# A fused scan, expert and quantised feed-forward kernel: ten entries per batch for the second scan's projections, and the first gate and the routing in one block

## What is computed

```python
# layer 0
x = x + silu(layernorm(x)) * ssm(ctx)        # the scan reads the context, not x
logits = layernorm(x) @ gate_w.T             # 16 experts, 4 chosen per token
x = x + sigmoid(...) * shared_ffn(xn) + sum_e coef_e * expert_e(xn)
# layer 1
x = x + silu(layernorm(x)) * ssm(ctx)        # a second scan of the same context
x = x + quantised_ffn(layernorm(x))

def ssm(h):                                  # per batch of 512 steps, 512 channels, 16 states
    u     = silu(causal_conv4(in_proj(h)))
    dt, B, C = split(x_proj(u))
    delta = softplus(dt_proj(dt) + bias)
    state = state * exp(delta * A) + delta * u * B
    y     = sum_n(state * C) + D * u
```

## Time and profile before

| | |
|---|---|
| median of 3 runs | 2226.88 us |
| the profiled execution | 2235.07 us, its span 2233.3 us |
| mean granted TensorE clock | 0.869 of 2.4 GHz |
| busy: TensorE, VectorE, GpSimd, ScalarE | 74%, 79%, 60%, 52% of the span |
| first gate | 648.4 to 725.9 us |
| routing | 727.7 to 788 us |
| block with the 168 slots | from 789.8 us |

### The profile page before, as it was taken

The page is one execution under the profiler, slowest core; times in us unless marked ns, Lnnn a source line. Parts: engine busy times, 40 slices in busy tenths (PEclk is TensorE's granted clock), DMA queues, the critical chain, the costliest instruction groups (busy, mean ns, idle before and its releaser), DMA issues. The chain is left out here.

```text
span 2233.3 us, 27174 instructions
## 1 busy us (share of the span) xinstructions
PE 1658.5 (74%) x8502; PEld 960.6 (43%) x8502; DVE 1757.4 (79%) x2275; ACT 1152.6 (52%) x1765; POOL 1341.3 (60%) x648
## 2 busy tenths in 40 slices
PE   4575766756638548999799998999989990016999
PEld 1122222222218525676467654666456660003554
DVE  2999999999955836998589867888588884856886
ACT  5676776766632014443444435555455550734776
POOL 2679878789952003887078945888268883652111
PEclk8688988879965569999999998999989995557999
DMA  7536546355542820000000442444424227640000
GB/s 256 196 137 214 178 159 211 135 190 194 175 146 76 160 68 11 10 10 15 34 10 1 149 140 102 148 165 161 156 102 160 82 76 295 182 155 6 20 25 29
DMA packets 127145, 264.63 MB, mean 118 GB/s; under 512 B 44547, under 2 KB 48387, under 8 KB 121795
## 3 DMA queue, kind: packets, MB, share of 16 engines
q1 hardware_dynamic: 93890, 184.24, 24.6%
q0 software_dynamic: 11520, 37.76, 5.7%
q10 hardware_dynamic: 21600, 40.90, 4.9%
HBM read 180.41 MB, written 82.44 MB: 118 GB/s over the span
## 5 line engine op out<-in xcount | busy, mean ns | idle before, releaser
L476 POOL TENSOR_TENSOR ssm_hs<-ssm_hs,ssm_Cs 128x1024 f32<-128x1024 f32 x128 | 313.9, 2461 | 89.5 <-DVE ssm_hs L443 89.5
L476 POOL TENSOR_TENSOR moe_hs<-moe_hs,moe_Cs 128x1024 f32<-128x1024 f32 x128 | 301.5, 2355 | 98.4 <-DVE moe_hs L443 97.5
L443 DVE TENSOR_TENSOR_SCAN moe_hs<-moe_dA,moe_bu 128x1024 f32<-128x1024 f32 x128 | 292.5, 2285 | 20.0 <-ACT moe_dA L357 10.2
L466 POOL TENSOR_TENSOR moe_U<-moe_U,moe_hs 128x1024 f32<-128x1024 f32 x128 | 302.2, 2361 | 5.9
L443 DVE TENSOR_TENSOR_SCAN ssm_hs<-ssm_dA,ssm_bu 128x1024 f32<-128x1024 f32 x128 | 291.6, 2278 | 0.1
L290 PE MATMUL ssm_pY<-ssm_hs,ssm_ident 128*128 128x512 f32 x512 | 275.5, 666 | 4.2 <-POOL ssm_hs L476 4.2
L1238 PE MATMUL moe_pgu<-moe_xsh,all_Wreg 128*128 128x256 f16 x1408 | 255.5, 280 | 12.8 <-DVE moe_hsl L1483 11.3
L1288 PE MATMUL moe_pgu<-all_Wreg,moe_xth 128*128 x1280 | 243.7, 313 | 0.0
L699 POOL TENSOR_TENSOR ssm_wlo<-ssm_wst,ssm_whi 128x1360 f16<-128x1360 f32 x64 | 190.3, 2973 | 45.7 <-ACT ssm_wst L635 45.7
L357 ACT ACTIVATE ssm_dA<-ssm_dlt,ssm_A 128x511 f32<-128x511 f32 x256 | 168.0, 710 | 63.2 <-DVE ssm_hs L443 60.0
L1238 PE MATMUL moe_pgu<-moe_xsl,all_Wreg 128*128 128x256 f16 x704 | 197.1, 280 | 0.0
(11 more groups left out here) (246 smaller groups left out, 3490.6 us busy)
## 6 DMA issues: line engine op xcount, KB each, us to landing
ssm_wst<-in_w_all SPq DMA_DIRECT2D x64, 680.0 KB, 5.0
w_hi<-ssm_whi SPq DMA_DIRECT2D x64, 340.0 KB, 2.3
w_lo<-ssm_wlo SPq DMA_DIRECT2D x64, 340.0 KB, 3.1
y_d<-moe_yo ACTq DMA_DIRECT2D x80, 256.0 KB, 3.1
all_Wreg<-w_hi SPq DMA_DIRECT2D x16, 1088.0 KB, 5.8
all_Wreg<-w_lo SPq DMA_DIRECT2D x16, 1088.0 KB, 8.7
ssm_Cs<-c_d SPq DMA_DIRECT2D x64, 256.0 KB, 5.4
gate_Y<-y_ssm ACTq DMA_DIRECT2D x8, 1024.0 KB, 9.2
```

Source lines behind the costliest of these rows:

```text
L443: self.nc.vector.tensor_tensor_scan(self.hs[:, j, :, :].rearrange("p k t -> p (k t)"), self.dA[:, q, :, :].rearrange("p k t -> p (k t)"), ...
L466: self.nc.gpsimd.tensor_tensor(Y, Y, self.hs[:, j, :, :], ALU.add).then_inc(self.acc_done, 1)
L476: self.nc.gpsimd.tensor_tensor(self.hs[:, j, :, :], self.hs[:, j, :, :], self.Cs[:, i:i + 1, :].to_broadcast([P, HC, L]), ALU.mult)\
```

## The change

Two parts.

1. PRO goes from 5 to 10, so PER is 42, the entries are 168 and each slot has one. Entries 0 to 3 hold one channel chunk each, entry 4 the Silu, entry 5 the x-projection, entries 6 and 7 the dt matmuls with Abs and Relu, and from 6 to 9 the rest by halves. The x-projection writes into pB instead of the first bank of `bu`; the convolution waits for GpSimd's sums by single steps.
2. `gate` with l = 0 and `routing` become one block, `gate_and_routing`. The constants are loaded at the start of it, with the weights of four chunks of the shared expert; the other chunks' loads stand between the stores of xn. G has 8 tiles instead of 16. The one-hot tiles and their source are f16. The table of the slots' experts comes from two small matmuls. `gate` stays for the second layer.

```diff
+    def bank_x(self):
+        return self.pw[0] if self.alone else self.pB[:]
+    def bank_dt(self, b, c):
+        return self.bank(b, c + 1 if self.alone else c)
...
-        if c == n - 1:
+        if c == n - 1 and self.alone:
             pe.wait_ge(self.bc_split, 5 * (b + 1))
-            if self.alone:
-                pe.wait_ge(self.cf_rdy, b + 1)
+            pe.wait_ge(self.cf_rdy, b + 1)
...
             if not self.alone:
-                act.wait_ge(self.acc_done, b * STEPS + R)
+                act.wait_ge(self.acc_done, b * STEPS + R - 3 + c // 2)
...
-        PRO = 5
+        PRO = 10
...
-                    if at == 0 or at == 1:
-                        S.pe_in(pe, b, 2 * at)
-                        S.pe_in(pe, b, 2 * at + 1)
+                    if at is not None and at < KC:
+                        S.pe_in(pe, b, at)
...
-                    if at == 2:
+                    if at == 5:
                         S.pe_x(pe, b)
-                    if at == 3:
-                        S.pe_dt(pe, b, 0)
-                        S.pe_dt(pe, b, 1)
+                    if at in (6, 7):
+                        for c in range(2):
+                            S.pe_dt(pe, b, 2 * (at - 6) + c)
...
+                    if at == 6:
+                        S.act_dt(act, b)
+                    if at in (7, 8):
+                        S.act_e(act, b, at - 7)
+                    if at in (8, 9):
+                        S.act_ln(act, b, at - 8)
                     if g >= 2:
                         y_evac(g - 2)
...
+                    if at is not None and at < KC:
+                        S.act_conv(act, b, at)
+                    if at == 2 and b:
+                        S.store_y(act, y_ssm, b - 1)
+                    if at == 3 and b + 1 < B:
+                        S.load_ctx(act, b + 1)
+                    if at == 4:
+                        S.act_u(act, b)
+                    if at in (6, 7):
+                        for c in range(2):
+                            S.act_z(act, b, 2 * (at - 6) + c)
...
+                    if at is not None and at < KC:
+                        S.dve_conv(dve, b, at)
+                    if at == 6:
                         S.dve_split(dve, b)
+                    if at in (7, 8):
+                        S.dve_t(dve, b, at - 7)
+                    if at in (8, 9):
+                        S.dve_delta(dve, b, at - 8)
+                        S.dve_du(dve, b, at - 8)
```

In the new block:

```diff
+def gate_and_routing(nc, d, X, y_ssm, r):
...
-        G = m.sb("G", [P, TT, L])
+        G = m.sb("G", [P, TT // 2, L])
...
-        ohp = m.sb("ohp", [P, 4, P])
-        ohs = m.sb("ohs", [P, 4, NSTEP])
+        ohp = m.sb("ohp", [P, 4, P], F16)
+        ohs = m.sb("ohs", [P, 4, NSTEP], F16)
...
+        colh = m.sb("colh", [P, P], F16)
...
+                for c in range(4):
+                    shared(c)
+                for i in range(TT):
+                    sp.wait_ge(xn_rdy, i + 1)
+                    sp.dma_start(r["xn_d"][i * P:(i + 1) * P, :], xn[:, i % 4, :]).then_inc(xn_out[i % 4], 16)
+                    if i + 4 < CSH:
+                        shared(i + 4)
...
+                    if i >= TT // 2:
+                        act.wait_ge(yg_rdy, i - TT // 2 + 1)
...
+                V.tensor_copy(r["first"][:], start[0:1, :])
+                own(V.tensor_scalar(begun[:, 0, :], start[:], tok[:, 0:1], None, ALU.is_le))
+                own(V.tensor_tensor(begun[:, 1, :], begun[:, 0, :], turn[:], ALU.mult))
+                V.reduce_sum(sew[:], begun[:], AX.X).then_inc(se_rdy, 1)
                 for g in range(TT * TOPK):
...
+                    V.tensor_scalar(ohp[:, g % 4, :], colh[:], pp[:, i, k:k + 1], None, ALU.is_equal)
+                    V.tensor_scalar(ohs[:, g % 4, :], colh[:, 0:NSTEP], stf[:, i, k:k + 1], tok[:, i:i + 1],
                                     ALU.is_equal, ALU.mult).then_inc(oh_rdy, 1)
...
+                dve.wait_ge(tab_rdy, 1)
+                V.tensor_copy(r["tab"][0:1, :, :], ptab[:, 0:2 * NSTEP].rearrange("p (a n) -> p a n", a=2))
...
+                pe.wait_ge(se_rdy, 1)
+                for q in range(2):
+                    mm = nc.tensor.matmul(ptab[:, q * NSTEP:(q + 1) * NSTEP], sew[:, q:q + 1], ident[:, 0:NSTEP],
+                                          start=True, stop=True)
+                mm.then_inc(tab_rdy, 1)
```

More of the change, by code:

```diff
@@ L717, in gate @@
+def gate_and_routing(nc, d, X, y_ssm, r):
+    with ExitStack() as ctx:
+        m = Mem(nc, ctx, "gate0")
         ident = m.sb("ident", [P, P])
@@ L750, in gate @@
         lg_out = m.sem("lg_out")
+        tri = m.sb("tri", [P, P])
+        ones = m.sb("ones", [P, P])
+        e_of = m.sb("e_of", [P, E])
+        thr = m.sb("thr", [P, TT])
+        col = m.sb("col", [P, P])
+        tok = m.sb("tok", [P, TT])
+        ex = m.sb("ex", [P, TT, E])
+        mx = m.sb("mx", [P, TT])
+        sm = m.sb("sm", [P, TT])
+        ri = m.sb("ri", [P, TT])
+        i8 = m.sb("i8", [P, TT, 8], U32)
+        idf = m.sb("idf", [P, TT, 8])
+        oh = m.sb("oh", [P, TOPK, TT, E])
+        M = m.sb("M", [P, TT, E])
+        base = m.sb("base", [P, TT, E])
+        cnt = m.sb("cnt", [P, TT, E])
+        off = m.sb("off", [P, TT + 1, E])
+        cmp = m.sb("cmp", [P, E, TT])
+        nt = m.sb("nt", [P, E])
+        incl = m.sb("incl", [P, E])
+        start = m.sb("start", [P, E])
+        one_e = m.sb("one_e", [P, E])
+        pos = m.sb("pos", [P, TT, TOPK])
+        posi = m.sb("posi", [P, TT, TOPK], I32)
+        sti = m.sb("sti", [P, TT, TOPK], I32)
+        stf = m.sb("stf", [P, TT, TOPK])
+        pp = m.sb("pp", [P, TT, TOPK])
+        ohp = m.sb("ohp", [P, 4, P], F16)
+        ohs = m.sb("ohs", [P, 4, NSTEP], F16)
+        turn = m.sb("turn", [P, E])
+        begun = m.sb("begun", [P, 2, E])
+        sew = m.sb("sew", [P, 2])
+        colh = m.sb("colh", [P, P], F16)
+        flat = [t[:].rearrange("p k t -> p (k t)") for t in pt]
+        pr_, pc, pi, ptab = flat[0][:, 0:TT * E], flat[1][:, 0:TT * E], flat[2][:, 0:NSTEP], flat[3][0:1, :]
+        r_loaded = m.sem("r_loaded")
+        mx_rdy = m.sem("mx_rdy")
+        e_rdy = m.sem("e_rdy")
+        se_rdy = m.sem("se_rdy")
+        tab_rdy = m.sem("tab_rdy")
+        m_rdy = m.sem("m_rdy")
+        rk_rdy = m.sem("rk_rdy")
+        oh_rdy = m.sem("oh_rdy")
+        oh_used = m.sem("oh_used")
+        step = m.sem("step")
+        fin = m.sem("fin")
         with nc.Block() as block:
@@ L1063, in _, with second, evac @@
                 dve.wait_ge(oh_used, TT * TOPK)
                 own(V.tensor_copy(r["idx"][:], pi[:]))
+            @block.scalar
+            def _(act):
+                for b in range(B):
+                    own = slice(b * KC, (b + 1) * KC)
+                    act.dma_start(Y[:, own, :], y_ssm.rearrange("(i p) t -> p i t", p=P)[:, own, :]).then_inc(y_in[b], 16)
+                act.wait_ge(eps_rdy, 1)
+                act.wait_ge(mv_rdy, TT)
+                nc.scalar.activation(sd[:, 0, :], mv[:, :, 1], ACT.Sqrt, bias=eps[:]).then_inc(sd_rdy, 1)
+                act.wait_ge(ln_rdy, 1)
+                for i in range(TT):
+                    if i >= TT // 2:
+                        act.wait_ge(yg_rdy, i - TT // 2 + 1)
+                    nc.scalar.activation(G[:, i % (TT // 2), :], X[:, i, :], ACT.Silu, bias=nmr[:, 0, i:i + 1],
+                                         scale=rstd[:, 0, i:i + 1]).then_inc(g_rdy, 1)
+                def second(b):
+                    own = slice(b * KC, (b + 1) * KC)
+                    act.wait_ge(mv_rdy, TT + (b + 1) * KC)
+                    nc.scalar.activation(sd[:, 1, own], r["mv"][:, own, 1], ACT.Sqrt, bias=eps[:]).then_inc(sd_rdy, 1)
+                def evac(b):
+                    for c in range(KC):
+                        i = b * KC + c
+                        act.wait_ge(tn_rdy, i + 1)
+                        if i >= 4:
+                            act.wait_ge(lg_rdy, i - 3)
+                        nc.scalar.copy(xT[:, i % 4, :, :], pn[i % 2][:]).then_inc(xT_rdy, 1)
+                second(0)
+                second(1)
+                for b in range(B):
+                    evac(b)
+                    if b + 2 < B:
+                        second(b + 2)
+                act.wait_ge(lg_rdy, TT)
+                nc.scalar.copy(r["logit"][:], plog[:, :, 0:E + 1]).then_inc(lg_out, 1)
+                act.wait_ge(mx_rdy, 1)
+                nc.scalar.activation(ex[:], ex[:], ACT.Exp).then_inc(e_rdy, 1)
+                nc.scalar.activation(r["sig"][:], r["logit"][:, :, E], ACT.Sigmoid).then_inc(fin, 1)
@@ L1524, in _ @@
                         S.dve_bu(dve, b, half, s)
-                    if at == 4:
-                        for h in range(2):
-                            S.dve_t(dve, b, h)
                     if g <= 0 and slot:
@@ L1943, in bass_program @@
         }
-        gate(nc, 0, d, X, y_ssm, r)
         with nc.sbuf_tensor("all_Wreg", [P, 2 * CSH * WC], F16) as Wreg:
```

(2 more changed lines are left out.)

360 lines of the change are left out of this document (151 added, 209 removed).

## The result

The changed kernel takes 2217.66 us, the median of 5 runs (2214.28 to 2223.25), beside 2228.55 for the kernel before (5 runs, 2226.09 to 2229.55): a ratio of 0.9948, interval 0.9933 to 0.9962.

What follows compares the result with a forecast made beforehand. It took TensorE to bound expert slots, with TensorE and VectorE both near their limit in shared slots. Entries +0.4 and gate and routing -1.1 sum to -0.7 us, so 2226 us was predicted, range 2211 to 2241.

Steps and rivals of the forecast that it cites:

- the tail of the first projections: Shared slots, wait after the last projection slot's tanh until the first scan: 12.4 us.
- the casts in a run of scans: Shared scan runs: two casts of 0.69 and two residual adds of 0.74 per 11 slots add 0.26 us per slot.
- what the held stores cost: Gate: xn stores wait behind chunk loads in SyncE's queue, delaying the logits by 11.7 us, bounds +7 to +15.
- the walk: 168-slot block, costed from scan to scan: +5.8, -25.9, +22.7 and -2.2 us, together +0.4.
- 31 x 5.04 = 156.3: Run of 32 scans in shared slots: 31 gaps of 4.79 plus 0.26 us for casts and adds.
- The gaps: Ten projection entries between batches' scans: 68.9 us in shared slots, 85.4 from batch 1 to 2, 91.8 in expert slots.
- 31 x 6.51 = 201.8: Run of 32 scans in expert slots: 31 gaps of 6.51 us, with TensorE full.
- tails vanish: Rival for the projections' tails: chains overlap better than walked, -23 us, 2204 at full price, 2212 at half; chance 0.18.
- The long scan runs hold VectorE and GpSimd above 5.04: Rival for shared scan runs: at 5.3 us per slot +17, 2243; decides from 5.1 on; chance 0.20.
- 20 empty slots were what let VectorE and GpSimd recover: Shared phase: removing the empty slots offsets some 30 us less of projection stalls.
- Store 7 is issued at 716: Gate, SyncE's queue: 28.3 us of load issue and eight stores of 0.5 put store 7 there, landing 2.5 later.
- the stores aren't held up: Rival for the gate: SyncE issues loads faster than in the old routing, -11.7 us, 2214; chance 0.16.

Runs made afterwards that it cites:

- e1: The ten projection entries per batch with the old gate and routing, against the kernel before: 2217.28 us, ratio 0.9946.
- e2: The merged gate and routing with the old five entries per batch, against the kernel before: 2233.40 us, ratio 1.0019.
- e11: The changed kernel measured again, nothing altered, beside the kernel before: 2217.60 us, ratio 0.9954.
- e5: e3 plus one 128x512 f32 VectorE copy behind each of the 64 shared-phase scans: 2226.58 us, ratio 0.9979 to the kernel before.
- e7: e3 plus one 128x512 f32 VectorE copy behind each of the 64 expert-phase scans: 2200.68 us, ratio 0.9859 to the kernel before.
- e6: e3 plus one 128x256 f32 GpSimd product in each of the 64 shared-phase scan slots: 2206.13 us, ratio 0.9887 to the kernel before.
- e10: The kernel before with its 148 entries in the first 148 slots, the 20 empty slots moved to the end: 2278.35 us, ratio 1.0214.
- e3: The changed kernel with shared chunk loads 4 to 10 issued behind all sixteen xn stores: 2201.58 us, ratio 0.9879 to the kernel before.
- e9: The changed kernel with all shared chunk loads issued first by SyncE and xn stores by ScalarE: 2200.48 us, ratio 0.9868 to the kernel before.
- e8: e3 with Exp of both halves in entry 8, Ln and delta of both in entry 9: 2217.65 us, ratio 0.9940 to the kernel before.

## Why the prediction came out as it did

The number came inside the range partly by luck. I forecast no change and 11 us were gained. By the runs, the entries gave -11.5 (e1) where I had +0.4, and gate and routing gave +4 to +5 (e2) where I had -1.1: both signs were wrong, and the two misses, 12 us and about 5.5 us, went opposite ways. The mechanisms were right in the main. What failed is the size of three terms: the tail of the first projections, the casts in a run of scans, and what the held stores cost.

**The entries: forecast +0.4, measured -6.5 in the trace of after, -11.7 in e11, -11.5 us by e1's runs.** Against the walk, with e11's scans in brackets where they differ from after's:
- From the first tanh to the first scan I had 66.3 (878.6 - 812.3); it is 62.0, so 4.3 less. Up to the tenth tanh 53.9 were forecast and 54.5 came. The term that failed is the tail, "12.4, longer since a slot has 3.9 us instead of 6.3 to hide it": 7.5.
- "31 x 5.04 = 156.3": 152.7 and 152.2. This view of VectorE (start, us) shows why:

```profile
945.59 2.29 DVE L450 TENSOR_TENSOR_SCAN moe_hs<-moe_dA,moe_bu 128x1024 f32<-128x1024 f32 x1 [0.27 <-ACT moe_dA L364]
...
949.70 0.42 DVE L1567 TENSOR_TENSOR moe_hsl<-moe_pgu,moe_hsh 128x256 f16<-128x256 f32 x1
950.38 2.29 DVE L450 TENSOR_TENSOR_SCAN moe_hs<-moe_dA,moe_bu 128x1024 f32<-128x1024 f32 x1 [0.27 <-ACT moe_dA L364]
...
953.36 0.68 DVE L1553 SCALAR_TENSOR_TENSOR moe_xsl<-moe_px,moe_xsh 128x512 f16<-128x512 f32 x1
...
955.08 0.41 DVE L1567 TENSOR_TENSOR moe_hsl<-moe_pgu,moe_hsh 128x256 f16<-128x256 f32 x1
955.42 2.27 DVE L450 TENSOR_TENSOR_SCAN moe_hs<-moe_dA,moe_bu 128x1024 f32<-128x1024 f32 x1
```

Without a cast scans stand 4.79 apart, and the scan waits for dA, as it did in the earlier trace rows: it starts 0.68 behind the cast of 949.70, and 0.34 behind that of 955.08, when it doesn't wait. So 4.79 isn't "VectorE back to back"; about 0.34 of it is free. The cast of 0.68 stands behind the product L1562 (953.01), so ScalarE's Exp run beside it, and the next operation starts 0.59 behind it (953.95); 0.34 goes into the wait and 0.25 is added (5.04). The two residual adds of a slot make it 5.75, 0.96 for the two. I had added 0.69 and 0.74 in full, 0.26 per slot; 0.13 came (4.92 on the mean). Over the two runs that is 3.6 and 4.1.
- The gaps: 68.9 forecast, 69.9; 91.8, 91.7; 85.4, 86.1 (82.8 at full clock). The tails were right in sum there, but lie in entries 7 to 9 rather than behind the last: 8.1 for 12.4 in the first gap, and 5.2 more before it.
- 31 x 6.51 = 201.8: 203.0. From scan 96 to the last tanh, 204.8 forecast: 207.2 (204.3 in e11).

The structure held: the shared phase loses, the expert phase gains, VectorE sets the one (e5), TensorE the other (e7), and the rival "tails vanish" named the direction (2204 to 2212), though what fell was 5 us of the first tail and half of the added casts and adds. "The long scan runs hold VectorE and GpSimd above 5.04" was wrong; the point was 5.1, and it is 4.92. Its argument was GpSimd's 4.7 of 4.79, and e6 shows that this share isn't a limit while there are buffers between. "20 empty slots were what let VectorE and GpSimd recover" fits e10, where filling them costs 82 us in the shared phase, and I had its price only through the count of scans.

**Gate and routing: forecast -1.1.** The traces and the runs say different things. By the traces, start to logits: forecast +11.7, measured +12.5 (+8.6 in e11); from the logits to the first tanh: forecast -12.8 from the sum of the terms, measured -14.2 (86.8 to 72.6), of which the f16 tiles 3.5. "Store 7 is issued at 716" came at 714.5, tile 11 was copied at 719.9 for 720.2. But this agreement is luck, since it rests on a slow base: in the profiled execution of before, TensorE ran at a lower clock in the router (last section). e1, with the same gate, has 71.6 where before has 77.1, and against 71.6 the delay is 14 to 18, not 11.7. That is the term that was too small: with it the sum is +1 to +5 instead of -1.1, and e2's runs have +4 to +5. The held stores cost 14 to 21 us by the traces (85.7 to 89.6 against 68.3 to 71.6) and 16 by the runs. "Stores are held up by loads issued between them" was the right mechanism, at a higher price, and "the stores aren't held up" fell.

The sum of the two, -0.7, missed 10 us: the entries missed by more than that, and the gate took back a part. The best that do no added work are e3 and e9 at 2201, 27 us below before and 16 below the changed kernel.

## To carry to other kernels

Before loads are put ahead in a queue, look at who waits for what stands behind them: here the loads of seven chunks, put between stores, took back all that loading ahead had won, since VectorE needed those stores to land. Two engines with the same busy share need not both set the pace: here one had a few buffers between itself and the next user and fell behind without being felt. A small dummy operation, on one of them per run, tells them apart. Work put into a bounded phase should go in pieces that leave no engine waiting for a long one behind them: that was worth 11 us here, and by e8 it was worth two more table loads per batch.
